# Large tiles at one SBUF offset, two places for queries, reordered first tiles, W_q's low parts on another engine, and the last residuals in the tokens' ring

## The chip, the cores and the metric

One core of one Trainium2 chip runs the kernel. The metric is the device time of one execution in microseconds (us). Engines are named as the profile names them: PE (TensorE matmuls), PEld (its weight loads), DVE (VectorE), ACT (ScalarE), POOL (GpSimd), SP (the queue that issues most DMAs).

## The reference

A conditioned linear attention over x of shape (2, 2048, 512), with 8 heads of 64 channels, all in float32:

```
xn = ln(x, ln_w, ln_b)
q = xn @ Wq + bq
k = xn @ Wk + bk + (1.0 - src_mask) * -1000000.0
q = softmax(q.reshape(b, t, h, dh), axis=-1)
k = softmax(k.reshape(b, t, h, dh), axis=1)
v = ((xn @ Wv + bv) * src_mask).reshape(b, t, h, dh)
att = einsum('bnhd,bnhl->bhdl', k, v)
y = einsum('bnhd,bhdl->bnhl', q, att).reshape(b, t, d)
scale, shift = split(silu(emb) @ W_emb + b_emb, 2)
hh = ln(y, ln2_w, ln2_b) * (1.0 + scale) + shift
out = x + silu(hh) @ W_out + b_out
```

## The kernel before

Tokens are worked in tiles of 128, 16 tiles for each of the two batch elements (b is 0 or 1, a tile of both together is m = 16 b + n). Four products take most of PE's time: K (`product_k`, normalised tokens by W_k), Q (`product_q`, by W_q), G (`product_g`, exponentials of the keys by masked tokens, summed over all tiles of a batch element) and O (`product_out`, the output). Each operand of them is split in a high and a low part of type float32r, and each product is three matmuls of 512 columns (high by high, high by low, low by high; L1154 to L1156), four times for a tile: 12 matmuls for each tile and product, 32 x 12 x 4 = 1,536 in all. A matmul has a stationary 128x128 block, loaded first, and a moving operand of 512 columns. In the profile's rows "ps<-wk_hi,zT_hi", the first name is what moves and the second what is stationary.

- K and Q: stationary `zT` (the turned tokens), moving `wk` or `wq`. 768 matmuls.
- G: stationary `zm` (masked tokens), moving `ek` (exponentials). 384 matmuls.
- O: moving `wo`; stationary `h`, which has no tiles of its own: below m = `HT` = 12 it stands in `zm` or `ek` (144 matmuls), from 12 on in `zT` when m % 4 is 0 or 1 (120) and in the tiles of `wk`, free by then, when m % 4 is 2 or 3 (120).

Besides, PE turns tiles (four 128x128 transposes of L1159 each), multiplies queries with the state (L1330) and sums exponentials (L1255).

The other engines: ACT makes normalised tokens, exponentials and high parts (`zT_high`, `ek_high`, `zm_high`, `h_high`, all by L306) and `scale_shift` (four pieces of L407 and a tanh, L412). DVE makes sums with biases, maxima, statistics and low parts (`q_add` L762, `q_top` L767, `k_less_max` L798, `masked_z` L779, `zm_low` L793, `ek_low` L803, `silu` L916, `out_tile` L922). POOL subtracts the maximum from queries (`q_shift` L577), makes `h_low` (L586) and adds b_out to the residual (`add_bias` L590).

Nothing schedules this at run time: every engine has its own list of instructions, in the order in which its code is written, and waits on semaphores. So an instruction that waits holds up all that stand behind it on its engine. The stages in order are: start (weights split while the first tokens come), K and Q of batch element 0, G of 0, a stage with K and Q of 1 beside the outputs 0 to 10, the turn to G of 1 (`k_less_max`, the last query tile, output 11), G of 1, and the outputs 12 to 31.

Details that the change touches:

- `qs`, the query tile between DVE, POOL and ACT, has one place: `q_add` waits for the exponential of the tile before (`dve.wait_ge(s["q_exp"], m)`).
- `product_g(b, 0)` writes four banks in the order 0, 2, 1, 3. Bank 1 waits for `q_sum` of the last query tile (the bank was that tile's), and for b = 1 bank 3 waits for `o_ok` of output 11 (`pe.wait_ge(s["o_ok"], HT)`), which is DVE's `out_tile(HT - 1)`, which needs POOL's `add_bias(HT - 1)`.
- Residuals stand in `res`, three places in turn: load, `add_bias`, `out_tile` adds the product in place, store, and only then the load of the tile three later (`refill`).
- Tiles of SBUF are given addresses in the order in which they are declared, each from a multiple of 32 bytes. In the program before, the weights (`wk_hi` to `wo_lo`) start 128 bytes past a multiple of 2,048 in each partition, `x_in`, `zT`, `kf` and `eq` 1,952 past one, `zm`, `ek`, `y`, `eqT`, `u`, `th`, `res` and `att` 2,016 past one.

Of the kernel before, what the change touches and what calls it, by code (L numbers as in the profile page):

```python
# [19 lines left out]
def cond_linear_attention(nc, x, cond, mask, ln_w, ln_b, wq, bq, wk, bk, wv, bv, w_emb, b_emb,  # L20
# [44 lines left out]
    with ExitStack() as ctx:  # L65
# [22 lines left out]
        part = sb("part", [P, P])  # L88
        ones = sb("ones", [P, 32])
# [7 lines left out]

        x_in = sb("x_in", [P, XR, D])  # L100
        zT_hi, zT_lo = sb("zT_hi", [P, 2, NB, P], F32R), sb("zT_lo", [P, 2, NB, P], F32R)

        kf = sb("kf", [P, T, D])
        eq = sb("eq", [P, T, D])
        qs = sb("qs", [P, D])
        qmax = sb("qmax", [P, H])
        km = sb("km", [P, D])
        kcol = sb("kcol", [P, NB])

        zm_hi, zm_lo = sb("zm_hi", [P, HI, D], F32R), sb("zm_lo", [P, LO, D], F32R)  # L110
        ek_hi, ek_lo = sb("ek_hi", [P, HI, D], F32R), sb("ek_lo", [P, LO, D], F32R)
        y = sb("y", [P, YR, D])
# [20 lines left out]
        yst_ps = [in_psum(yst[k], 64 * k) for k in range(2)]  # L133
        x_r, x_shift = sb("x_r", [P, T]), sb("x_shift", [P, T])
# [47 lines left out]
        def flat(t):  # L182
# [3 lines left out]
        wk_raw, wq_raw, wo_raw = y[:, 0:4], kf[:, 4:8], eq[:, 6:10]  # L186
        bias_part, bv_all = kf[:, 15, :], kf[:, 14, :]
# [9 lines left out]
            wk_hi_ok wk_lo_ok wq_hi_ok wq_lo_ok wv_ok wo_hi_ok wo_lo_ok  # L197
# [9 lines left out]
        res_in = [sem(f"res_in{t}") for t in range(RR)]  # L207
        stored = [sem(f"stored{t}") for t in range(RR)]
# [18 lines left out]
        def _(sp):  # L227
# [7 lines left out]

            def store(m):
                sp.wait_ge(s["o_ok"], m + 1)
                sp.dma_start(out_tok[:, m, :], res[:, m % RR, :]).then_inc(stored[m % RR], 16)

            def refill(m):  # L240

                if m >= 0 and m + RR < B * T:
                    sp.wait_ge(stored[m % RR], 16 * (m // RR + 1))
                    load_res(m + RR)
# [59 lines left out]
        def _(act):  # L304
# [26 lines left out]
            def exp_q(b, n):  # L331
# [4 lines left out]
                act.activation(eq[:, n, :], qs[:], ACT.Exp).then_inc(s["q_exp"], 1)  # L336
# [189 lines left out]
            scale_shift(HT)  # L526
            zm_high(1, 1)
            exp_k(1, 1)
            ek_high(1, 1)
            exp_q(1, T - 1)  # L530
            h_high(HT)
            scale_shift(HT + 1)

            def last_outputs(n):
                if n == 2:
# [32 lines left out]
        def _(pool):  # L568
# [19 lines left out]
            def add_bias(m):  # L588
                pool.wait_ge(res_in[m % RR], 16 * (m // RR + 1))
                pool.tensor_tensor(res[:, m % RR, :], res[:, m % RR, :], bo_all[:], ALU.add).then_inc(s["res_b"], 1)  # L590
# [61 lines left out]
        def _(dve):  # L652
# [850 lines left out]
```

## Time and profile before

| | |
|---|---|
| median of 3 runs | 483.63 us (482.94 to 485.74) |
| the profiled execution's own time | 484.99 us |
| its span, first to last instruction | 483.2 us |
| PE busy | 464.2 us (96%) |
| DVE busy | 363.3 us (75%) |
| ACT busy | 263.1 us (54%) |
| POOL busy | 132.8 us (27%) |
| mean granted clock of TensorE | 0.996 |

Busy time of PE counts each matmul to its modelled end, and consecutive ones overlap; so how fast PE runs is read from the starts of consecutive rows, not from the busy share.

### The profile page before, as it was taken

How to read it: one execution, taken by the hardware profiler on the slowest of the kernel's cores; microseconds unless marked ns; L12 is line 12 of the kernel's file. 1: busy time of each engine (PE TensorE's matmuls, PEld its weight loads, DVE VectorE, ACT ScalarE, POOL GpSimd, SP SyncE). 2: the span in 40 equal slices, each digit the busy share in tenths (PEclk: the TensorE clock that was granted, in tenths of full speed). 3: DMA queues.
4: the chain of work that ended last, by engine and by line, in shares of the span. 5: the costliest groups of instructions: out<-in, count | busy, mean ns of one | idle time of the engine just before them, and what ended most of it. 6: DMA issues, size and time to landing. Idle time of an engine off the chain costs nothing.

```text
span 483.2 us, 7324 instructions
## 1 busy us (share of the span) xinstructions
PE 464.2 (96%) x2478; PEld 371.8 (77%) x2478; DVE 363.3 (75%) x879; ACT 263.1 (54%) x485; POOL 132.8 (27%) x148
## 2 busy tenths in 40 slices
PE   4999999998899999999999999999899999989997
PEld 2677876885688878888888888888588868878875
DVE  6979976775878956979678658675988628888963
ACT  5333332321788523347555655655988814777882
POOL 0013311120200000104223233332410133676675
PEclk9999999999999999999999999999999999999999
DMA  8945310112133200110213212121322000233354
GB/s 284 356 168 207 121 43 7 46 46 102 43 121 98 88 26 19 45 43 1 82 28 132 84 49 87 45 87 45 131 85 69 0 1 23 89 131 124 123 172 149
DMA packets 23093, 43.50 MB, mean 90 GB/s; under 512 B 1992, under 2 KB 2064, under 8 KB 23056
## 3 DMA queue, kind: packets, MB, share of 16 engines
q1 hardware_dynamic: 21968, 40.93, 24.7%
q10 hardware_dynamic: 1088, 2.10, 1.2%
q8 instruction: 20, 0.33, 0.3%
q14 instruction: 17, 0.14, 0.1%
HBM read 34.64 MB, written 8.39 MB: 89 GB/s over the span
## 4 chain that ended last, share of the span: by engine, by line
PE 83%; DVE 8%; ACT 3%; issue 3%; POOL 1%; DMA 1%; POOLq 0%; DVEq 0%; ACTq 0%
PE ps L1154 21%; PE ps L1156 21%; PE ps L1155 21%; PE ps L1159 8%; PE ps L1330 5%; ACT ps L407 2%; PE ps L1255 1%; PE ps L1308 1%; DVE th L916 1%; PE ps L1227 1%; PE ps L1208 1%; DMA x_in<-in_x_dram 1%; DVE yst_raw L661 1%; DVE kf L798 1%; DVE qs L762 1%
## 5 line engine op out<-in xcount | busy, mean ns | idle before, releaser
L577 POOL TENSOR_TENSOR qs<-qs,qmax 128x512 f32<-128x512 f32 x32 | 35.9, 1122 | 192.8 <-DVE qmax L767 192.8
L1154 PE MATMUL ps<-ek_hi,zm_hi 128*128 128x512 f32 x128 | 51.5, 402 | 3.7 <-DVE ek_lo L803 2.1
L1154 PE MATMUL ps<-wk_hi,zT_hi 128*128 128x512 f32 x124 | 51.5, 415 | 1.7 <-DVE kf L748 1.7
L1154 PE MATMUL ps<-wq_hi,zT_hi 128*128 128x512 f32 x128 | 52.3, 409 | 0.3 <-DVE qs L762 0.3
L1156 PE MATMUL ps<-wq_hi,zT_lo 128*128 128x512 f32 x128 | 50.6, 395 | 0.0
L1155 PE MATMUL ps<-wq_lo,zT_hi 128*128 128x512 f32 x128 | 50.5, 395 | 0.0
L306 ACT ACTIVATE zT_hi<-ps 128x512 fp32r<-128x512 f32 x32 | 19.1, 596 | 57.6 <-PE ps L1159 57.6
L1156 PE MATMUL ps<-ek_hi,zm_lo 128*128 128x512 f32 x128 | 50.4, 394 | 0.0
L1155 PE MATMUL ps<-ek_lo,zm_hi 128*128 128x512 f32 x128 | 50.3, 393 | 0.0
L1156 PE MATMUL ps<-wk_hi,zT_lo 128*128 128x512 f32 x124 | 49.0, 395 | 0.0
L1155 PE MATMUL ps<-wk_lo,zT_hi 128*128 128x512 f32 x124 | 49.0, 395 | 0.0
L762 DVE TENSOR_TENSOR qs<-ps,bq_all 128x512 f32<-128x512 f32 x32 | 22.0, 689 | 32.9 <-PE ps L1156 30.5
L590 POOL TENSOR_TENSOR res<-res,bo_all 128x512 f32<-128x512 f32 x32 | 42.4, 1327 | 14.9 <-PE ps L1156 8.8
L306 ACT ACTIVATE eqT<-ps 128x512 f32<-128x512 f32 x17 | 10.2, 600 | 42.2 <-PE ps L1159 42.2
L1154 PEld LDWEIGHTS ps<-ek_hi,zm_hi 128*128 128x128 f32 x128 | 24.4, 191 | 11.0 <-DVE ek_lo L803 3.3
L748 DVE SCALAR_TENSOR_TENSOR kf<-ps,pen,bk_all 128x512 f32<-128x512 f32 x32 | 23.8, 746 | 11.6 <-PE ps L1156 11.5
L793 DVE TENSOR_TENSOR zm_lo<-x_in,zm_hi 128x512 fp32r<-128x512 f32 x32 | 22.6, 706 | 11.8 <-PE ps L1156 10.9
L922 DVE TENSOR_TENSOR res<-ps,res 128x512 f32<-128x512 f32 x32 | 21.9, 685 | 11.0 <-PE ps L1156 6.3
L336 ACT ACTIVATE eq<-qs 128x512 f32<-128x512 f32 x32 | 20.0, 625 | 17.3 <-POOL qs L577 17.3
L1154 PEld LDWEIGHTS ps<-wq_hi,zT_hi 128*128 128x128 f32 x128 | 24.1, 188 | 6.3 <-issue 0.8
L1156 PEld LDWEIGHTS ps<-wq_hi,zT_lo 128*128 128x128 f32 x128 | 24.0, 188 | 5.8
L1154 PEld LDWEIGHTS ps<-wk_hi,zT_hi 128*128 128x128 f32 x124 | 23.3, 188 | 6.6 <-issue 2.3
(230 smaller groups left out, 1163.2 us busy)
## 6 DMA issues: line engine op xcount, KB each, us to landing
x_in<-in_x_dram SPq DMA_DIRECT2D x32, 512.0 KB, 3.5
res<-in_x_dram SPq DMA_DIRECT2D x32, 256.0 KB, 2.8
out_dram<-res SPq DMA_DIRECT2D x32, 256.0 KB, 2.0
y<-in_L_cond_Wk_dram ACTq DMA_DIRECT2D x2, 512.0 KB, 5.3
kf<-in_L_cond_Wq_dram ACTq DMA_DIRECT2D x1, 1024.0 KB, 8.1
eq<-in_L_cond_W_out_dram SPq DMA_DIRECT2D x1, 1024.0 KB, 8.5
wv_mod<-in_L_cond_Wv_dram SPq DMA_DIRECT2D x1, 1024.0 KB, 10.7
eq<-in_L_cond_W_emb_dram SPq DMA_DIRECT2D x4, 256.0 KB, 4.4
```

Of the source, the lines that this page charges most:

```text
L306: act.activation(o, i, ACT.Copy, scale=scale).then_inc(s[done], 1)
L577: pool.tensor_tensor(q_heads, q_heads, qmax[:].unsqueeze(2).broadcast_to([P, H, DH]), ALU.subtract).then_inc(s["q_shift"], 1)
L590: pool.tensor_tensor(res[:, m % RR, :], res[:, m % RR, :], bo_all[:], ALU.add).then_inc(s["res_b"], 1)
L748: dve.scalar_tensor_tensor(out=kf[:, n, :], in0=ps[:, OB if m == 1 else KB, :], scalar=pen[:, m:m + 1], in1=bk_all[:], op0=ALU.add, op1=AL ...
L762: dve.tensor_tensor(qs[:], ps[:, TB if m == 1 else QB, :], bq_all[:], ALU.add).then_inc(s["q_sum"], 1)
L793: dve.tensor_tensor(zm_lo[:, n % LO, :], x_in[:, at, :], zm_hi[:, n % HI, :].bitcast(F32), ALU.subtract).then_inc(s["zm_lo_ok"], 1)
L922: dve.tensor_tensor(res[:, m % RR, :], o_bank(m), res[:, m % RR, :], ALU.add).then_inc(s["o_ok"], 1)
L1154: pe.matmul(o, a[0], bb[0], start=start, stop=False)
L1155: pe.matmul(o, a[0], bb[1], start=False, stop=False)
L1156: return pe.matmul(o, a[1], bb[0], start=False, stop=stop)
L1159: return pe.transpose(o, i, ident[0:i.shape[0], 0:i.shape[0]])
L1330: last = pe.matmul(ps[:, bank, at:at + YW], eqT[:, m % 2, q, :] if m < T else blk(eq[:, m - T, :], q), att[:, q, :], start=True, stop=True)
```

## The change

Six edits stand in the diff. The large tiles are declared ahead of the small ones, and `qs` grows by a tile, so that every large tile from `x_in` to `att` starts 1,152 bytes past a multiple of 2,048, and the weights stay at 128: all of them are 128 past a multiple of 1,024. `qs` and `qmax` have two places. The low parts of W_q are POOL's, which takes the scaled weight from ACT (`wq_scaled`, a second copy) and subtracts the high part; the statistics of tokens 2 to 5 stand in PSUM, in the bank of the queries, so the first query product waits for them. At the turn to G of batch element 1 and in the last outputs several steps stand in another order. In the start, `key_bias(1)` stands ahead of the first transposes. The residuals of outputs 24 to 31 are loaded in pairs into `x_in`, all at once when G is done, and stored from there.

```diff
+        x_in = sb("x_in", [P, XR, D])
+        zT_hi, zT_lo = sb("zT_hi", [P, 2, NB, P], F32R), sb("zT_lo", [P, 2, NB, P], F32R)
+        kf = sb("kf", [P, T, D])
+        eq = sb("eq", [P, T, D])
+        qs = sb("qs", [P, 2, D])
...
         ones = sb("ones", [P, 32])
...
-        qs = sb("qs", [P, D])
-        qmax = sb("qmax", [P, H])
+        qmax = sb("qmax", [P, 2, H])
...
+        xst_ps = in_psum(xst, 128)
...
+        def res_of(m):
+            return res[:, m % RR, :] if m < 2 * T - XR else x_in[:, m - 2 * T + XR, :]
...
+        wq_scaled = eq[:, 0:4]
...
+            sp.wait_ge(s["g_ps"], 2 * T)
+            for m in range(2 * T - XR, 2 * T, 2):
+                load_late(m)
             for m in range(HT, 2 * T):
                 store(m)
...
+            zT_high(0, 0)
             act.wait_ge(s["wk_in1"], 16)
             wk_high(2)
-            zT_high(0, 0)
             wk_high(3)
...
                 wq_high(f)
+                copy(wq_scaled[:, f, :], wq_raw[:, f, :], "wq_scaled", ln_weight(f))
...
+            for f in range(NB):
+                pool.wait_ge(s["wq_scaled"], f + 1)
+                pool.tensor_tensor(wq_lo[:, f, :], wq_scaled[:, f, :], wq_hi[:, f, :].bitcast(F32),
+                                   ALU.subtract).then_inc(s["wq_lo_ok"], 1)
...
-                if m:
-                    dve.wait_ge(s["q_exp"], m)
+                if m > 1:
+                    dve.wait_ge(s["q_exp"], m - 1)
...
             masked_z(1, 0)
             k_less_max(1, 0)
+            masked_z(1, 1)
+            k_less_max(1, 1)
             out_tile(HT - 2)
-            k_less_max(1, 1)
             zm_low(1, 0)
             q_add(1, T - 1)
             ek_low(1, 0)
             q_top(1, T - 1)
-            masked_z(1, 1)
+            out_tile(HT - 1)
+            zm_low(1, 1)
+            ek_low(1, 1)
             k_less_max(1, 2)
             masked_z(1, 2)
             silu(HT)
-            out_tile(HT - 1)
-            zm_low(1, 1)
-            ek_low(1, 1)
...
+            silu(T + 2)
             out_tile(HT + 3)
...
+                if m == 0:
+                    pe.wait_ge(s["x_norm"], 2)
...
             key_bias(0)
+            key_bias(1)
             turn_z(0, 0)
             turn_z(0, 1)
-            key_bias(1)
```

On ACT the same turn has `scale_shift(HT)` behind `ek_high(1, 1)` in place of ahead of `zm_high(1, 1)`, and `h_high(HT)`, `scale_shift(HT + 1)` and `h_high(HT + 1)` move from the turn into steps 1, 3 and 5 of G.

**First place, the turn to G of batch element 1, on DVE.** The list starts at the maximum of the keys (`kcol`). `x_in<-x_in` is `masked_z`, `kf<-kf,ps` is `k_less_max`, `res<-ps,res` is `out_tile`, `th<-th,u` is `silu`. Before:

```order
L779 TENSOR_SCALAR x_in<-x_in,xm_r,xm_shift 128x512
L798 TENSOR_TENSOR kf<-kf,ps 128x512
L779 TENSOR_SCALAR x_in<-x_in,xm_r,xm_shift 128x512
L916 SCALAR_TENSOR_TENSOR th<-th,u 128x512
L922 TENSOR_TENSOR res<-ps,res 128x512
L793 TENSOR_TENSOR zm_lo<-x_in,zm_hi 128x512
L803 TENSOR_TENSOR ek_lo<-kf,ek_hi 128x512
```

In the changed program, from `q_top` of the last query tile on:

```order
L801 TENSOR_REDUCE qmax<-qs 128x8
L956 TENSOR_TENSOR res<-ps,res 128x512
L827 TENSOR_TENSOR zm_lo<-x_in,zm_hi 128x512
L837 TENSOR_TENSOR ek_lo<-kf,ek_hi 128x512
L832 TENSOR_TENSOR kf<-kf,ps 128x512
L813 TENSOR_SCALAR x_in<-x_in,xm_r,xm_shift 128x512
L950 SCALAR_TENSOR_TENSOR th<-th,u 128x512
```

`out_tile(11)` and the low parts of state tile 1 moved ahead of `k_less_max` and `masked_z` of tile 2 and of `silu(12)`.

**Second place, the last outputs, on DVE**, around output 15 (`res<-ps,res`) and output 18's `silu` (`th<-th,ps`). Before:

```order
L862 TENSOR_TENSOR kf<-ps,rec 128x512
L922 TENSOR_TENSOR res<-ps,res 128x512
L661 BN_STATS yst_raw<-kf 128x6 x2
L916 SCALAR_TENSOR_TENSOR th<-th,ps 128x512
L858 RECIPROCAL rec<-ps 128x8
```

and in the changed program:

```order
L896 TENSOR_TENSOR kf<-ps,rec 128x512
L950 SCALAR_TENSOR_TENSOR th<-th,ps 128x512
L956 TENSOR_TENSOR res<-ps,res 128x512
L693 BN_STATS yst_raw<-kf 128x6 x2
L892 RECIPROCAL rec<-ps 128x8
```

`silu(18)` moved ahead of `out_tile(15)` and of two statistics.

## Rows read from the trace of the kernel before

**Rows 1.** The page, part 1: busy time, share of the span, instructions.
```profile
PE 464.2 (96%) x2478; PEld 371.8 (77%) x2478; DVE 363.3 (75%) x879; ACT 263.1 (54%) x485; POOL 132.8 (27%) x148
```

**Rows 2.** The page, part 4: the chain that ended last, by engine.
```profile
PE 83%; DVE 8%; ACT 3%; issue 3%; POOL 1%; DMA 1%; POOLq 0%; DVEq 0%; ACTq 0%
```

**Rows 3.** Timeline of PE: start, duration (us); a K product, then G.
```profile
55.02 0.39 PE L1155 MATMUL ps<-wk_lo,zT_hi 128*128 128x512 f32 x1
...
57.34 0.40 PE L1156 MATMUL ps<-wk_hi,zT_lo 128*128 128x512 f32 x1
...
139.76 0.39 PE L1155 MATMUL ps<-ek_lo,zm_hi 128*128 128x512 f32 x1
...
144.97 0.39 PE L1154 MATMUL ps<-ek_hi,zm_hi 128*128 128x512 f32 x1
```

**Rows 4.** Timeline of PE: matmuls 2 and 12 of three O products.
```profile
434.10 0.40 PE L1155 MATMUL ps<-wo_lo,wk_hi 128*128 128x512 f32 x1
...
436.41 0.40 PE L1156 MATMUL ps<-wo_hi,wk_lo 128*128 128x512 f32 x1
...
438.21 0.39 PE L1155 MATMUL ps<-wo_lo,zT_hi 128*128 128x512 f32 x1
...
440.54 0.40 PE L1156 MATMUL ps<-wo_hi,zT_lo 128*128 128x512 f32 x1
...
477.20 0.40 PE L1155 MATMUL ps<-wo_lo,wk_hi 128*128 128x512 f32 x1
...
479.47 0.39 PE L1156 MATMUL ps<-wo_hi,wk_lo 128*128 128x512 f32 x1
```

**Rows 5.** Timeline, start of G of batch element 0; in brackets idle before.
```profile
124.68 0.69 DVE L762 TENSOR_TENSOR qs<-ps,bq_all 128x512 f32<-128x512 f32 x1 [1.67 <-ACT eq L336]
...
125.43 0.50 PE L1154 MATMUL ps<-ek_hi,zm_hi 128*128 128x512 f32 x1 [0.69 <-DVE qs L762]
...
129.82 0.68 DVE L803 TENSOR_TENSOR ek_lo<-kf,ek_hi 128x512 fp32r<-128x512 f32 x1
...
130.55 0.50 PE L1154 MATMUL ps<-ek_hi,zm_hi 128*128 128x512 f32 x1 [0.73 <-DVE ek_lo L803]
```

**Rows 6.** Timeline, turn to G of batch element 1.
```profile
343.52 1.49 POOL L590 TENSOR_TENSOR res<-res,bo_all 128x512 f32<-128x512 f32 x1
...
346.21 0.50 PE L1154 MATMUL ps<-ek_hi,zm_hi 128*128 128x512 f32 x1 [0.96 <-DVE res L922]
...
346.68 1.77 DVE L803 TENSOR_TENSOR ek_lo<-kf,ek_hi 128x512 fp32r<-128x512 f32 x1
...
348.50 0.79 PE L1154 MATMUL ps<-ek_hi,zm_hi 128*128 128x512 f32 x1 [1.33 <-DVE ek_lo L803]
...
352.10 0.40 PE L1154 MATMUL ps<-ek_hi,zm_hi 128*128 128x512 f32 x1
```

**Rows 7.** Windows 349:350: busy PE, PEld, DVE, ACT, POOL; granted clock; DMA.
```profile
349.00:350.00 1.00, 1.00 (x4) 0.71 (x4) 0.70 (x3) 1.00 (x3) 0.00 (x0) 0.50 1.05 408
```

**Rows 8.** Timeline, the last outputs, around output 18's `silu`.
```profile
421.15 0.60 ACT L412 ACTIVATE th<-ps 128x512 f32<-128x512 f32 x1
...
424.31 0.67 DVE L916 SCALAR_TENSOR_TENSOR th<-th,ps 128x512 f32<-128x512 f32 x1
...
428.39 0.66 PE L1159 MATMUL ps<-ident,kf 128*128 128x128 f32 x4 [1.55 <-ACT kf L395]
```

**Rows 9.** Timeline, the start of the kernel.
```profile
9.21 1.97 PE L1159 MATMUL ps<-ident,x_in 128*128 128x128 f32 x8 [0.66 <-ACT x_in L321]
...
21.94 0.50 PE L1154 MATMUL ps<-wq_hi,zT_hi 128*128 128x512 f32 x1
```

**Rows 10.** Groups by line, POOL: busy us, mean ns.
```profile
L623 POOL TENSOR_TENSOR wo_lo<-eq,wo_hi 128x512 fp32r<-128x512 f32 x4 | 5.2, 1298 | 0.0
```

**Rows 11.** Timeline, the stall in the fifth token tile.
```profile
42.65 0.48 PE L1154 MATMUL ps<-wk_hi,zT_hi 128*128 128x512 f32 x1 [0.70 <-DVE kf L748]
```

**Rows 12.** Timeline, the end.
```profile
480.00 0.69 DVE L922 TENSOR_TENSOR res<-ps,res 128x512 f32<-128x512 f32 x1 [1.15 <-POOL res L590]
```

More of the change, by code:

```diff
@@ L88, in cond_linear_attention @@
         part = sb("part", [P, P])
+        x_in = sb("x_in", [P, XR, D])
[3 more added lines that the diff above has]
+        qs = sb("qs", [P, 2, D])
+        km = sb("km", [P, D])
+        zm_hi, zm_lo = sb("zm_hi", [P, HI, D], F32R), sb("zm_lo", [P, LO, D], F32R)
+        ek_hi, ek_lo = sb("ek_hi", [P, HI, D], F32R), sb("ek_lo", [P, LO, D], F32R)
+        y = sb("y", [P, YR, D])
+        eqT = sb("eqT", [P, 2, NB, P])
+        u, th = sb("u", [P, D]), sb("th", [P, D])
+        res = sb("res", [P, RR, D])
+        att = sb("att", [P, NB, YW])
         ones = sb("ones", [P, 32])
@@ L207, in cond_linear_attention @@
         res_in = [sem(f"res_in{t}") for t in range(RR)]
+        res_late = [sem(f"res_late{t}") for t in range(XR // 2)]
         stored = [sem(f"stored{t}") for t in range(RR)]
@@ L234, in load_res, with load_late @@
                 sp.dma_start(res[:, m % RR, :], x_tok[:, m, :]).then_inc(res_in[m % RR], 16)
+            def load_late(m):
+                at = m - 2 * T + XR
+                sp.dma_start(x_in[:, at:at + 2, :], x_tok[:, m:m + 2, :]).then_inc(res_late[at // 2], 16)
             def store(m):
                 sp.wait_ge(s["o_ok"], m + 1)
[L238 removed]
+                sp.dma_start(out_tok[:, m, :], res_of(m)).then_inc(stored[m % RR], 16)
             def refill(m):
[L242 removed]
+                if m >= 0 and m + RR < B * T - XR:
                     sp.wait_ge(stored[m % RR], 16 * (m // RR + 1))
@@ L335, in exp_q @@
                     act.wait_ge(s["eqT_ps"], n + 1)
-                act.activation(eq[:, n, :], qs[:], ACT.Exp).then_inc(s["q_exp"], 1)
+                elif n < NB:
+                    act.wait_ge(s["wq_lo_ok"], n + 1)
+                act.activation(eq[:, n, :], qs[:, n % 2, :], ACT.Exp).then_inc(s["q_exp"], 1)
             def exp_k(b, n):
@@ L529, in _ @@
             ek_high(1, 1)
+            scale_shift(HT)
             exp_q(1, T - 1)
-            h_high(HT)
-            scale_shift(HT + 1)
             def last_outputs(n):
-                if n == 2:
+                if n == 1:
+                    h_high(HT)
+                if n == 3:
+                    scale_shift(HT + 1)
+                if n == 5:
                     h_high(HT + 1)
@@ L588, in add_bias @@
             def add_bias(m):
-                pool.wait_ge(res_in[m % RR], 16 * (m // RR + 1))
-                pool.tensor_tensor(res[:, m % RR, :], res[:, m % RR, :], bo_all[:], ALU.add).then_inc(s["res_b"], 1)
+                if m < 2 * T - XR:
+                    pool.wait_ge(res_in[m % RR], 16 * (m // RR + 1))
+                else:
+                    pool.wait_ge(res_late[(m - 2 * T + XR) // 2], 16)
+                pool.tensor_tensor(res_of(m), res_of(m), bo_all[:], ALU.add).then_inc(s["res_b"], 1)
             steps_done = [0]
@@ L696, in xst_of @@
             def xst_of(b, c):
+                if b == 0 and c == 1:
+                    return xst_ps
                 return yst[0] if b and c == 0 else xst
```

36 lines of the change are left out of this document (11 added, 25 removed).

## Prediction

> **What bounds the kernel now.** I read the busy times first: PE is busy for 96% of the span, DVE for 75% [rows 1]. Then the chain that ended last: 83% of it lies on PE and 8% on DVE [rows 2]. So two things can shorten the kernel: a smaller distance between PE's matmuls, and the removal of places where PE stands still. For the first I read the timeline of PE, from start to start inside a product, since busy time overlaps. For the second I went through the timeline for rows of PE that carry an idle time.
>
> **The distance between matmuls.** In a K product ten steps take 57.34 - 55.02 = 2.32 us, 0.232 each; in G 23 steps take 144.97 - 139.76 = 5.21 us, 0.2265 each [rows 3]. Both are 128x128 by 512 columns of the same type. In the outputs the same code runs with the stationary operand in two places: out of `zT` ten steps take 2.33 us (0.233), out of `wk` 2.31 (0.231) in a slow product and 2.27 (0.227) in a fast one [rows 4]. What differs is where the tiles stand. `wk` and `wo` start at the same byte modulo 2,048, and so do `zm` and `ek`, the pair of G; `zT` and the weights do not. So rows of one kernel, one of them with nothing else changed, say that a pair at the same offset is faster by 2 to 6 ns. The change gives every pair the same offset modulo 1,024. Blocks inside a tile lie 512 bytes apart, so `wk` by `wo` products already contain distances of 512, 1,024 and 1,536 bytes; a distance of 1,024 is nothing new.
>
> Of the 1,536 matmuls 384 (G) and 120 (O out of `wk`) have equal offsets already. 1,032 are left; I leave out 24 of the fifth token tile, where PE waits for DVE [rows 11], and 24 of outputs 28 and 29, which are paced by ACT and DVE. I take the middle of the fast and the slow product, 0.229, against 0.233: 984 x 0.004 = **3.9 us**. The ends are 984 x 0.002 = 2.0 and 984 x 0.006 = 5.9.
>
> The Trainium skill speaks against this term. "TensorE: Matmul & The Clock Gate", section "Step-by-step: what each phase is for", says that PE reads the moving operand and the weights through two independent ports, so that loading weights takes no read bandwidth from a running matmul; by that rule where the tiles stand changes nothing and the term would be 0. The rows show a difference by place, so I give that rule a rival and not the forecast.
>
> **Two places for queries.** At the start of G of batch element 0, `q_add` of the last query tile waited 1.67 us for the exponential of the tile before, and PE's bank 1 waited 0.69 us for it [rows 5]. With two places it waits for the exponential two tiles back, long done, so it goes as soon as its product is there, which PE finishes before it begins G, six matmuls ahead of bank 1. So PE's wait of 0.69 goes, 0.8 with the restart, and its start moves from 125.43 to about 124.6. Behind it on DVE everything comes some 1.5 us sooner, `ek_low` of tile 2 too, which PE awaited for 0.73 us [rows 5]. With PE 0.8 sooner as well, `ek_low`'s end of 130.5 has to come to 128.8; its chain (`k_less_max` on DVE, exponential and two high parts on ACT) comes 1.3 to 1.6 sooner. I take 1.5 of the 1.7 us: **1.5 us**. The ends are 0.8 (the second stall stays) and 1.7.
>
> **The turn to G of 1.** Before, PE waited 0.96 us for `out_tile(11)`, ran three matmuls and waited 1.33 us for `ek_low(1)`, which took 1.77 us where other rows of its kind take 0.68 [rows 5, 6]. Then PE's granted clock was 0.50 [rows 7], its lower level of 1.2 GHz, after 0.96 + 1.33 us of idleness: from 348.50 to 352.10 there are nine matmuls, 3.60 us in place of 9 x 0.227 = 2.04, a loss of 1.56. In the new order `out_tile(11)` stands right behind `q_top`, but it also needs POOL's `add_bias(11)`, which ended at 343.52 + 1.49 = 345.01 [rows 6] and stands behind `q_shift` of the last query tile, hence behind `q_top`, which is now half a microsecond later for the `masked_z(1)` ahead of it. DVE is then idle, so POOL's two instructions should run at their undisturbed lengths and give most of that back. So `out_tile` starts at 345.1 to 345.4, PE goes on at about 345.9 (0.3 sooner), `zm_low(1)` and `ek_low(1)` follow at 0.6 to 0.7 each and end at 347.1, and `product_g(1, 1)` starts at 347.15 in place of 348.50: 1.35. The clock should hold, since the idle stretches shrink to 0.75 and 0.5 us: 1.56 more. What is late next is tile 2: its `k_less_max`, `masked_z`, `silu(12)` and `k_less_max(3)` now stand behind, then ACT's chain; I find `ek_low(2)` ending at 350.5, when PE wants it at 349.8, and a rest of 0.35 at tile 3, where the statistics' steps moved to steps 1 to 4. So 1.35 + 1.56 - 1.05 = **1.9 us**. The ends are 0 (the wait on POOL grows and the clock falls again) and 3.8, when no new wait comes.
>
> The Trainium skill, "SBUF — State Buffer", section "Who interferes with whom", says that a VectorE instruction with two SBUF inputs and a GpSimd instruction that reads SBUF exclude each other. The 1.77 us row agrees: POOL's `h_low(12)` ran beside it. By that rule `ek_low(1)` is free of it in the new order, since `silu(12)` comes later; a `silu` that is held up costs PE nothing there.
>
> **The last outputs.** Tanh of output 18 ended at 421.75, its `silu` ran at 424.31, and the chain from there through ACT (high part, `scale_shift`, `normalise_y`) let PE wait 1.55 us at 428.39 [rows 8]. `silu` moves ahead of three instructions, 1.8 us sooner, and PE finds its transpose ready. But the next `silu` then stands behind `out_tile(16)`, which waits for PE, and ACT is 0.9 us late for the transpose after it. I take **1.0 us**; the ends are 0.6 and 1.7.
>
> **The start.** `key_bias(1)` fills PE's idle 0.66 us [rows 9], and product K of tile 0 starts some 0.8 sooner; its third and fourth blocks wait for weights that ACT now makes later. I take **0.5 us**, ends 0 and 0.8. W_q's low parts cost nothing: ACT adds four copies of some 0.64 us between those of `wq_high`, which I let begin at 13.7, so the last is ready by 18.8; POOL subtracts four times at 1.3 [rows 10], over by 20.3, and PE's first query product came at 21.94 [rows 9]. The cover is 1 us; if it is gone, each late microsecond is one of PE's. The same holds for the new wait on the statistics, which I put at 20.4, since DVE is rid of four instructions. The DVE stall of 0.70 in the fifth tile stays [rows 11]: DVE is released by PE ahead of it, so its lead is lost.
>
> **The late residuals** are worth 0. Loads that waited for stores delayed `add_bias`, but at the end DVE's last sum began at 480.00 [rows 12] while PE's last matmul had started at 479.47 [rows 4] and lasted 0.39. Four more issues on SP before output 12's store lie in the sum of exponentials.
>
> **Sum.** 3.9 + 1.5 + 1.9 + 1.0 + 0.5 = 8.8 us. The profiled execution took 484.99 us (span 483.2), and would take 476.2. It lies 1.36 above the median of the runs, so for the median I predict 483.63 - 8.8 = **474.8 us**.
>
> **The rivals.**
> - The offset does nothing (the port rule above): gain 4.9, 478.7 us. For it: G stands in another stage, and a product's distance differs by 4 ns among products of the same pair. Against it: outputs out of `zT` and `wk` alternate in one stage. Chance 0.15.
> - The turn to G of 1 gains nothing, as DVE's list now stands still behind POOL: gain 6.9, 476.7 us. Chance 0.14. Both together and a late W_q leave less than 2.4: chance 0.05.
> - Everything at the fast end, with all pairs at 0.227: 5.9 + 1.7 + 3.8 + 1.7 + 0.8 = 13.9, 469.7 us. Chance 0.05.
> - Slower: the wait on POOL at the turn leaves PE's clock at 0.50 for much of G. At that level a matmul takes 0.427 in place of 0.227, so 47% of the time is lost. To end 2.4 us above before it has to eat 6.9 + 2.4 = 9.3 us, that is 20 us at half clock, against 3.3 before. Nothing in the rows shows such a stretch; PE works without a gap from the third tile on. Chance 0.03.
>
> The forecast itself has 0.58.
>
> **The numbers.** The range goes from 471.0 (most of the fast case left out) to 478.8, which takes in the first two rivals. A measurement here tells about 0.5% (2.4 us) from no change: faster by more than that 0.92, within it 0.05, slower 0.03.
>
> **What would show it.** K, Q and `zT` outputs at 0.227 to 0.231 from start to start; no idle PE row at bank 1 of `product_g(0, 0)`; no stretch at clock 0.50 in G of 1, but one wait of 0.7 us or so for `out_tile(11)` and one for `ek_low(2)`; the 1.55 us row gone and one of 0.9 in its place one output later. Distances of 0.233 in K and Q would make the largest term wrong, and a first query product later than 21.4 the one on W_q.

## Result and the profile after

The kernel before took 483.52 us in the median of 4 runs (482.94 to 485.74), the changed one 479.27 us (4 runs, 478.93 to 480.19). The ratio is 0.991, with a 95% interval of 0.9884 to 0.9937. So the change gained 4.3 us (0.6 to 1.2% by the interval) where I had forecast 8.8: the direction was right, the size was not, and the time lies outside my range (471.0 to 478.8). A second measurement of the same kernel beside others (e13 below) gave 479.32.

First the page after, parts 1 and 4, which answer to [rows 1, 2].

```profile
PE 459.6 (96%) x2478; PEld 369.9 (77%) x2478; DVE 359.7 (75%) x875; ACT 264.8 (55%) x489; POOL 137.4 (29%) x152
...
PE 80%; DVE 11%; issue 4%; ACT 2%; DMA 1%; POOL 0%; ACTq 0%; DVEq 0%
```

PE lost 4.6 us of busy time with the same number of matmuls. Some 1.6 of it is the stretch at half clock [rows 7], which is not there after the change; the rest says that a matmul got cheaper. But DVE's part of the chain rose from 8% to 11%, so PE waits for DVE in a new place. The timeline of PE in the changed kernel (start, duration, in brackets the idle time ahead and who ended it) shows where:

```profile
8.37 3.75 PE L1245 MATMUL ps<-y,cols 128*128 128x512 f32 x4 [3.89 <-DMA y<-in_L_cond_Wk_dram]
...
23.14 0.50 PE L1188 MATMUL ps<-wq_hi,zT_hi 128*128 128x512 f32 x1
...
118.92 0.60 PE L1193 MATMUL ps<-ident,kcol 128*128 128x128 f32 x4
...
128.83 0.50 PE L1188 MATMUL ps<-ek_hi,zm_hi 128*128 128x512 f32 x1 [0.21 <-DVE ek_lo L837]
...
333.00 0.65 PE L1193 MATMUL ps<-ident,kcol 128*128 128x128 f32 x4 [0.35 <-DVE kcol L806]
...
337.80 0.47 PE L1188 MATMUL ps<-wo_hi,ek_hi 128*128 128x512 f32 x1 [1.40 <-DVE res L956]
...
344.47 0.50 PE L1188 MATMUL ps<-ek_hi,zm_hi 128*128 128x512 f32 x1 [0.23 <-DVE ek_lo L837]
...
347.93 0.50 PE L1188 MATMUL ps<-ek_hi,zm_hi 128*128 128x512 f32 x1 [0.45 <-DVE ek_lo L837]
...
352.07 0.50 PE L1188 MATMUL ps<-ek_hi,zm_hi 128*128 128x512 f32 x1 [1.08 <-DVE ek_lo L837]
...
396.49 2.03 PE L1367 MATMUL ps<-att,eq 128*128 128x130 f32 x16 [0.30 <-ACT eq L324]
...
423.35 0.60 PE L1193 MATMUL ps<-ident,kf 128*128 128x128 f32 x4
...
474.80 0.39 PE L1190 MATMUL ps<-wo_hi,wk_lo 128*128 128x512 f32 x1
```

The reader is to see three things. At the start of G of batch element 0 the row at bank 1 [rows 5] is gone and the second stall shrank from 0.73 to 0.21. The wait of 1.55 us in the last outputs [rows 8] is gone. And at the turn to G of 1 the two waits of [rows 6] gave way to four: 1.40, 0.23, 0.45 and 1.08. The first of them is new, and DVE and POOL of the same kernel show what it is made of:

```profile
334.88 1.29 POOL L615 TENSOR_TENSOR ek_lo<-th,ek_hi 128x512 fp32r<-128x512 f32 x1 [5.76 <-ACT ek_hi L324]
...
335.10 1.35 DVE L813 TENSOR_SCALAR x_in<-x_in,xm_r,xm_shift 128x512 f32<-128x512 f32 x1
...
336.98 0.68 DVE L956 TENSOR_TENSOR res<-ps,res 128x512 f32<-128x512 f32 x1
...
340.12 1.05 POOL L606 TENSOR_TENSOR qs<-qs,qmax 128x512 f32<-128x512 f32 x1 [3.96 <-DVE qmax L801]
...
341.13 1.29 POOL L622 TENSOR_TENSOR res<-res,bo_all 128x512 f32<-128x512 f32 x1
...
342.52 0.69 DVE L956 TENSOR_TENSOR res<-ps,res 128x512 f32<-128x512 f32 x1 [2.48 <-POOL res L622]
...
344.93 0.55 DVE L813 TENSOR_SCALAR x_in<-x_in,xm_r,xm_shift 128x512 f32<-128x512 f32 x1
...
349.83 1.64 POOL L615 TENSOR_TENSOR zT_lo<-th,zT_hi 128x512 fp32r<-128x512 f32 x1 [7.40 <-ACT zT_hi L324]
...
350.24 1.78 DVE L837 TENSOR_TENSOR ek_lo<-kf,ek_hi 128x512 fp32r<-128x512 f32 x1
```

`out_tile(10)` (336.98) now stands behind `masked_z(1, 1)` (335.10) and a `k_less_max`, and PE's `product_out(11)` writes the bank that `out_tile(10)` has to read first. More than half of the wait of 1.40 comes from the length of `masked_z(1, 1)`: it took 1.35 us beside POOL's `h_low(11)` (334.88), where the next one (344.93), with nothing on POOL, took 0.55. The clock did hold, as I had said; the window that answers to [rows 7]:

```profile
349.00:350.00 1.00, 1.00 (x6) 0.82 (x5) 0.90 (x6) 1.00 (x3) 0.17 (x1) 1.00 0.00 0
```

To add the gains up I cut PE's timeline at five rows that every kernel has: its first bias product (6.51 us before), the turn of `kcol` of batch element 0 (119.13 before), the first product out of `att` (184.86), the turn of `kcol` of 1 (336.42), the first product out of `att` behind it (399.82), and the end of the last matmul.

| stretch of PE, us | before | after | difference |
|---|---|---|---|
| up to the first bias product | 6.51 | 8.37 | +1.86 |
| to `kcol` of 0 (start, K, Q) | 112.62 | 110.55 | -2.07 |
| to `att` of 0 (G of 0) | 65.73 | 64.12 | -1.61 |
| to `kcol` of 1 | 151.56 | 149.96 | -1.60 |
| to `att` of 1 (the turn, G of 1) | 63.40 | 63.49 | +0.09 |
| to the end (outputs) | 80.04 | 78.70 | -1.34 |
| end of the last matmul | 479.86 | 475.19 | -4.67 |

The first line is the landing of W_k's first half, 1.9 us later in this execution than in the one before; whether that is chance is taken up below.

### The profile page after: what moved, and what is told of

Read it like the earlier page. It is cut to its first block, busy times and chain, and to the rows that moved or that the text cites. A ratio compares the mean times of both kernels' runs of the same rounds, so it can differ in the third digit from the quotient of the medians.

```text
span 478.4 us, 7328 instructions
## 1 busy us (share of the span) xinstructions
PE 459.6 (96%) x2478; PEld 369.9 (77%) x2478; DVE 359.7 (75%) x875; ACT 264.8 (55%) x489; POOL 137.4 (29%) x152
## 4 chain that ended last, share of the span: by engine, by line
PE 80%; DVE 11%; issue 4%; ACT 2%; DMA 1%; POOL 0%; ACTq 0%; DVEq 0%
PE ps L1188 21%; PE ps L1190 21%; PE ps L1189 20%; PE ps L1193 8%; PE ps L1367 4%; PE ps L1292 1%; DMA y<-in_L_cond_Wk_dram 1%; PE ps L1245 1%; DVE kf L896 1%; DVE res L956 1%; DVE ek_lo L837 1%; ACT ps L428 1%; PE ps L1345 1%; PE ps L1264 1%; DVE th L950 1%
## 5 line engine op out<-in xcount | busy, mean ns | idle before, releaser
L622 POOL TENSOR_TENSOR res<-res,bo_all 128x512 f32<-128x512 f32 x24 | 31.6, 1319 | 11.8 <-PE ps L1190 8.8
L775 DVE TENSOR_TENSOR zT_lo<-ps,zT_hi 128x512 fp32r<-128x512 f32 x32 | 21.9, 686 | 8.5 <-ACT zT_hi L324 8.5
```

Source lines behind the costliest of these rows:

```text
L622: pool.tensor_tensor(res_of(m), res_of(m), bo_all[:], ALU.add).then_inc(s["res_b"], 1)
L775: dve.tensor_tensor(flat(zT_lo[:, n % 2]), z_bank(T * b + n), flat(zT_hi[:, n % 2]).bitcast(F32), ALU.subtract).then_inc(s["zT_lo_ok"], 1)
```

## The experiments

Times are medians of 4 to 12 runs, but e5, e6, e12, e15 and e16 ran once each. Every kernel was run beside the kernel before on the same chip, whose median was 483.6 to 484.6 us; the changed kernel itself was not run beside the others except in e13. So where two medians of different experiments lie within 1.5 us, I go by the stretches of PE's timeline. They repeat within 0.2 us from kernel to kernel wherever neither the code, the offsets nor the clock differ, except the first, which holds the start.

**e1: the order of declarations alone.** The kernel before with the new order of `sb(...)` lines and nothing else.

```diff
+        x_in = sb("x_in", [P, XR, D])
+        zT_hi, zT_lo = sb("zT_hi", ...), sb("zT_lo", ...)
...
         ones = sb("ones", [P, 32])
...
-        x_in = sb("x_in", [P, XR, D])
```

> The kernel before with only the declaration order of the tiles changed, so that all large tiles stand 128 bytes past a multiple of 1,024. If the offset is worth what the starts of matmuls in the changed kernel say (3.5 to 5 ns on about 1,000 matmuls), 479.6 us, and K, Q and zT outputs at 0.229 from start to start. If the pitch fell for another reason, 483.5 us and 0.233. For the start: if the new places make W_k's load slower, its first half lands at about 8.3 us; if that was chance of one run, at about 6.4.

Measured: 480.01 us, ratio 0.9924 (0.9896 to 0.9952), a gain of 3.9 us (2.3 to 5.0 by the interval). The offsets alone are worth most of the measured gain. In PE's timeline, from the first Q product on and without the stretch that holds the turn, they are worth 1.41 + 0.07 + 1.44 + 0.04 = 3.0 us against before. The stretch to `att` of 1 took 62.39 us here, with the old lists at the turn; that is 1.0 shorter than before and after.

**e2: everything but the order of declarations.** A filler of 32 bytes behind `qs` restores the old offsets although `qs` has grown.

```diff
-        x_in = sb("x_in", [P, XR, D])
+        ones = sb("ones", [P, 32])
```

> The changed kernel with the tiles at their old offsets. Offset theory: all other edits together are worth about 0.4 to 1 us, so 482.5 to 483 us, pitch 0.233 in K and Q. Rival, that the offset gives nothing: 479.3 us. W_k lands at about 6.4 us if the layout made it late in the changed kernel, at either time if it is chance.

Measured: 481.98 us, ratio 0.9955 (0.9938 to 0.9971), 1.9 us below before. Together with e1's 3.9 that would be 5.8, more than the whole change gained; with the 3.0 of the timeline it is 4.9. Its stretches were 111.70, 64.19, 151.57, 63.52 and 78.84: G of 0 and the outputs as after, the others longer by 1.15 and 1.61.

**e3: the sum of output 10 first again.** The changed kernel with one instruction of DVE moved.

```diff
+            out_tile(HT - 2)
             masked_z(1, 1)
             k_less_max(1, 1)
-            out_tile(HT - 2)
```

> The changed kernel with out_tile(10) again ahead of masked_z(1, 1) and k_less_max(1, 1). PE's wait of 1.40 us ahead of output 11's product should go. Theory that the turn hangs on POOL's add_bias(11) behind q_shift behind q_top: the time stays within 0.4 us of the changed kernel (479.3), since PE then waits for bank 3 some 1.4 us longer. Rival, that out_tile(10) alone cost the turn: 477.9 us.

Measured: 477.78 us, ratio 0.9868 (0.9842 to 0.9895). That is 1.5 us below the changed kernel and near the rival's 477.9, and my expectation that the time would come back at POOL was wrong. But the timeline does not bear the rival out in full, since the greater part of the 1.40 came back at ACT:

```profile
330.75 0.65 PE L1193 MATMUL ps<-ident,kcol 128*128 128x128 f32 x4 [0.35 <-DVE kcol L806]
...
338.22 0.63 PE L1193 MATMUL ps<-ident,y 128*128 128x128 f32 x4 [1.24 <-ACT u L428]
...
345.08 0.50 PE L1188 MATMUL ps<-ek_hi,zm_hi 128*128 128x512 f32 x1 [0.40 <-DVE ek_lo L837]
...
349.21 0.50 PE L1188 MATMUL ps<-ek_hi,zm_hi 128*128 128x512 f32 x1 [1.10 <-DVE ek_lo L837]
```

The wait of 1.40 at `product_out(11)` is gone and another of 1.24 stands behind that product: `turn_y(13)` wants the scratch `u`, and ACT's `scale_shift(12)` was moved behind three instructions of tile 1 by the change. In the changed kernel it was hidden under the wait of 1.40. The stretch to `att` of 1 shortened by only 0.6 (to 62.88). The other 0.9 is not in the turn; the first bias product came at 5.96 here against 8.37, so it may be the landing of the weights. That isn't shown.

**e4: POOL's bias ahead of its query shift.** e3, and:

```diff
                 if t == T - 1:
                     h_low(HT - 1)
+                    add_bias(HT - 1)
                 q_shift(1, t)
-            add_bias(HT - 1)
```

> As the kernel with out_tile(10) first, and POOL's add_bias(11) ahead of q_shift of the last query tile. Theory of the POOL chain: out_tile(11) follows its product, PE has no wait at bank 3, product_g(1, 1) starts 2 us sooner, and the POOL subtract that slowed ek_low(3) lies elsewhere: 476.3 to 477.3 us. Rival, that DVE's own list bounds the turn: 478.5 to 479.3 us.

Measured: 476.50 us, ratio 0.9844 (0.9814 to 0.9873). The time is as expected, and the stretch to `att` of 1 fell by 1.55 to 61.33. One part of the expectation failed: `ek_low(3)` still took 1.78 us beside POOL's `h_low(12)`.

**e7: ACT's `scale_shift(12)` ahead of tile 1 again.** e4, and:

```diff
+            scale_shift(HT)
             zm_high(1, 1)
             exp_k(1, 1)
             ek_high(1, 1)
-            scale_shift(HT)
```

> The kernel of e4 with ACT's scale_shift of output 12 back ahead of masked z's high part of tile 1, so that it ends at some 337.2 and not 338.8. First theory: PE's wait of 1.19 us for u of output 12 goes, but DVE has no idle row from there to ek_low of tile 3, so PE only meets that wait (0.63) grown to 1.4 to 1.8; gain over e4 0 to 0.4 us, 476.1 to 476.5. Rival: the wait is simply removed and everything behind it comes 1.2 us sooner, 475.3.

Measured: 476.35 us, ratio 0.9849 (0.9828 to 0.9869), the stretch to `att` of 1 61.30 against 61.33. The wait for `u` is gone, and nearly all of it came back as `ek_low`'s:

```profile
21.32 0.50 PE L1188 MATMUL ps<-wq_hi,zT_hi 128*128 128x512 f32 x1 [0.62 <-DVE x_shift L725]
...
344.11 0.50 PE L1188 MATMUL ps<-ek_hi,zm_hi 128*128 128x512 f32 x1 [0.40 <-DVE ek_lo L837]
...
348.24 0.50 PE L1188 MATMUL ps<-ek_hi,zm_hi 128*128 128x512 f32 x1 [1.11 <-DVE ek_lo L837]
```

(The first row belongs to the start, and comes up below.) In e4 the row that answers to the second has no idle time and the one that answers to the third 0.63. So by then DVE sets the pace of the turn, as a window of e4 (busy PE, PEld, DVE, ACT, POOL, then the clock) says in one figure, 7.00 of 7.00 us:

```profile
338.00:345.00 7.00, 6.07 (x29) 5.14 (x30) 7.00 (x12) 5.67 (x12) 1.04 (x1) 1.00 0.44 151
```

**e8: work out of DVE's way.** e7, with the four parts of `y_finish` on DVE and the high parts and `scale_shift` on ACT some tiles later:

```diff
-                if 1 <= n < 5:
-                    y_finish(T - 1, (n - 1,))
+                if 3 <= n < 7:
+                    y_finish(T - 1, (n - 3,))
...
-                if n == 1:
+                if n == 3:
                     h_high(HT)
-                if n == 3:
+                if n == 4:
                     scale_shift(HT + 1)
-                if n == 5:
+                if n == 6:
                     h_high(HT + 1)
```

> The kernel of e7 with work moved out of DVE's way in the first tiles of G of 1: the four parts of y_finish at tiles 3 to 6 and the high part of output 12 at tile 3, so that POOL's low part runs beside a later ek_low. If DVE's list is what bounds these tiles, the wait at tile 3 shrinks to below 0.4 us and the time is 1.0 to 1.5 us below e4 (475.0 to 475.5); if the contention with POOL only moves to a later tile and PE then waits there, it is the same as e7.

Measured: 476.29 us, ratio 0.9849 (0.9826 to 0.9873). In the profile the wait of 1.11 is gone, `ek_low` of tile 3 (347.29) took 0.69 us, and the stretch to `att` of 1 is 60.84, 0.46 below e7:

```profile
343.56 0.50 PE L1188 MATMUL ps<-ek_hi,zm_hi 128*128 128x512 f32 x1 [0.42 <-DVE ek_lo L837]
```

The medians don't tell e8 from e7, so the gain that I expected of it (1.0 to 1.5) isn't there; the trace shows 0.5.

**e9: the old lists at the turn.** The changed kernel with DVE's and ACT's lists of before at the turn to G of 1, the rest as changed; the part on DVE:

```diff
-            masked_z(1, 1)
-            k_less_max(1, 1)
             out_tile(HT - 2)
+            k_less_max(1, 1)
...
-            out_tile(HT - 1)
-            zm_low(1, 1)
-            ek_low(1, 1)
+            masked_z(1, 1)
...
             silu(HT)
+            out_tile(HT - 1)
+            zm_low(1, 1)
+            ek_low(1, 1)
```

> The changed kernel with the lists of ACT and DVE at the turn to G of 1 as they were before; the rest of the change stays. My prediction gave the new lists 1.9 us, by which this takes 481.2. The theory after the profiles: from the turn's transpose of kcol to the exponentials' sums it took 63.4 us with the new lists (after and e2), 62.4 with the old ones where no stretch at clock 0.50 came (e1) and 63.4 where it came (before). So the new lists cost 1.1 us in an ordinary run, and this takes 478.2. Rival: the old lists profit from neither, 479.3 as after.

Measured: 478.29 us, ratio 0.9868 (0.9841 to 0.9895). That is 1.0 us below the changed kernel (479.3), where my prediction had the new lists gain 1.9. The interval overlaps that of e13 (0.9868 to 0.9918), so the time alone rules out the gain but does not fix the cost; the stretches, 63.49 with the new lists and 62.39 with the old ones in e1, put it at 1.1. The profiled execution had the two old waits and behind them the low clock:

```profile
340.40 0.50 PE L1186 MATMUL ps<-ek_hi,zm_hi 128*128 128x512 f32 x1 [1.00 <-DVE res L954]
...
342.68 0.79 PE L1186 MATMUL ps<-ek_hi,zm_hi 128*128 128x512 f32 x1 [1.32 <-DVE ek_lo L835]
```

```profile
344.00:345.00 1.00, 1.00 (x4) 0.72 (x4) 1.00 (x3) 1.00 (x3) 0.00 (x0) 0.50 0.43 166
```

and its stretch to `att` of 1 took 63.52. In e1, with the same lists, the window just behind the stall reads

```profile
344.00:345.00 1.00, 0.78 (x3) 0.67 (x4) 0.76 (x2) 1.00 (x4) 0.00 (x0) 1.00 1.01 391
```

and the stretch took 62.39, although PE had stood for as long:

```profile
341.94 0.50 PE L1152 MATMUL ps<-ek_hi,zm_hi 128*128 128x512 f32 x1 [1.02 <-DVE res L920]
...
344.22 0.50 PE L1152 MATMUL ps<-ek_hi,zm_hi 128*128 128x512 f32 x1 [1.30 <-DVE ek_lo L801]
```

The six runs of e9 say the same of one program: three had a mean clock of 0.996 (477.85 to 479.20 us) and three of 0.999 or 1.000 (477.50 to 478.92). So the same lists fall to 0.50 in some executions and not in others.

**e10: the start of before.** W_q's low parts by DVE in place of POOL, no copies on ACT, `key_bias(1)` behind the two turns, and `x_finish(0, 1)` in its old place.

```diff
-                copy(wq_scaled[:, f, :], wq_raw[:, f, :], "wq_scaled", ln_weight(f))
...
+                weight_low(wq_lo, wq_raw, wq_hi, "wq", f)
...
-                if m == 0:
-                    pe.wait_ge(s["x_norm"], 2)
...
-            key_bias(1)
             turn_z(0, 0)
             turn_z(0, 1)
+            key_bias(1)
```

> The changed kernel with the start as it was: W_q's low parts by DVE from the raw weights, ACT without its four copies, key_bias(1) behind the two turns, the old place of the second chunk's statistics. My prediction gave the start 0.5 us: 479.8. By the profiles from PE's first bias product to the turn of kcol 0 the start is worth 0.6 to 0.9 us: 479.9 to 480.2. Rival: PE then waits for the statistics (0.6 us in e7) or W_q's parts as long as it gained, 479.3.

Measured: 478.70 us, ratio 0.9881 (0.9853 to 0.991). Not slower than the changed kernel, so the forecast gain of 0.5 is not there.

**e11: `silu` of output 18 back.**

```diff
-            silu(T + 2)
             out_tile(HT + 3)
...
-                if T < m < 2 * T - 2:
+                if m + 2 < 2 * T:
                     silu(m + 2)
```

> The changed kernel with the silu of output 18 back behind the sum of output 15. My prediction gave that step 1.0 us (0.6 to 1.7); by the profile of after the stretch of the outputs became 1.3 us shorter, so the time is 480.6. Rival: the wait is given back at the next output anyway, 479.3.

Measured: 480.03 us, ratio 0.9907 (0.9879 to 0.9934), 0.7 us above the changed kernel on other chips, and 1.3 above e10 on the same one. The times don't fix the size. The old wait is back, and the stretch of the outputs is 79.90 against 78.70:

```profile
423.31 0.66 PE L1192 MATMUL ps<-ident,kf 128*128 128x128 f32 x4 [1.57 <-ACT kf L416]
```

**e13 and e14: the changed kernel again, and e8 with the start of before.** e13 has no edit, and e14 is e8 with the edit of e10.

> The changed kernel itself, beside the others on the same chip. If the late landing of the first half of W_k (PE's first bias product at 8.37 us) was that execution's alone, the profile starts at 6 to 7.5 us and the median is 478.8 to 479.0; if it belongs to the change, it starts after 8 again and the median is 479.3.

> The kernel of e8 with the start of before, as in e10. If the new start is worth the predicted 0.5 us, it takes 476.8; if it gains nothing, 476.3; if PE's new wait for the statistics makes it cost 0.5, 475.8.

Measured: e13 479.32 us, ratio 0.9893 (0.9868 to 0.9918); e14 476.81 us, ratio 0.9845 (0.9819 to 0.9871), where e8 had 0.9849. With the start of before the best kernel is as fast as with the new one. In e13 PE's first bias product again came late, and the median is the one that I had named for a late landing that belongs to the change:

```profile
8.06 3.75 PE L1245 MATMUL ps<-y,cols 128*128 128x512 f32 x4 [3.32 <-DMA y<-in_L_cond_Wk_dram]
```

**e5, e6, e12, e15, e16: how equal the offsets must be.** The changed kernel with 32, 64, 512, 128 and 256 bytes of padding, which move `zT`, `zm` and `ek` together against the weights:

```diff
         part = sb("part", [P, P])
+        gap = sb("gap", [P, 8])
```

> The changed kernel with 32 bytes of padding ahead of x_in, so that zT, zm and ek stand 32 bytes away from the weights modulo 64, as they did before, while everything else about the new layout stays. If the phase modulo 64 bytes between the stationary and the moving tile is what costs, the start-to-start distance in K, Q and outputs by zT, zm or ek returns to 0.233 us (0.2292 after the change) and G, whose two tiles move together, stays at 0.2275; the time is about 3.9 us longer than after the change, near 483. If only larger distances (512 bytes and up) matter, the distances stay at 0.229.

> The same with 64 bytes of padding. If the phase modulo 64 bytes is what costs, all distances stay at 0.229 and the time at about 479.3. If the tiles must agree modulo 512 or 1,024 bytes, as my prediction put it, they return to 0.233 in K, Q and the outputs, and the time is near 483.

> The changed kernel with 512 bytes of padding ahead of x_in, one block's distance inside a tile. Products of wk and wo contain distances of 512, 1,024 and 1,536 bytes between the two operands and run at 0.229. If equality modulo 512 bytes is enough, K, Q and the outputs stay at 0.229 and the time at 479.3. If it is modulo 1,024, they return to 0.233 and the time to about 482, as with 32 and 64 bytes.

> The changed kernel with 128 bytes of padding ahead of x_in. If equality modulo 128 bytes is enough, K, Q and the outputs stay at 0.229 from start to start; if it takes 256 or 512, they are at 0.233.

> The same with 256 bytes. With e15 it brackets the step: 0.229 here and 0.233 in e15 is 256 bytes, 0.233 in both is 512, 0.229 in both is 128.

One product's distance varies (0.226 to 0.233 after the change), so I read the stretch from the first matmul of tile 0's Q product to the turn of `kcol`, which holds the 360 matmuls of tiles 1 to 15 and some others. The two rows of each kernel, with 64 bytes (e6), 128 (e15), 256 (e16) and 512 (e12):

```profile
21.58 0.50 PE L1189 MATMUL ps<-wq_hi,zT_hi 128*128 128x512 f32 x1
...
118.84 0.60 PE L1194 MATMUL ps<-ident,kcol 128*128 128x128 f32 x4
```

```profile
21.33 0.51 PE L1189 MATMUL ps<-wq_hi,zT_hi 128*128 128x512 f32 x1
...
118.44 0.60 PE L1194 MATMUL ps<-ident,kcol 128*128 128x128 f32 x4
```

```profile
21.56 0.50 PE L1189 MATMUL ps<-wq_hi,zT_hi 128*128 128x512 f32 x1
...
117.36 0.60 PE L1194 MATMUL ps<-ident,kcol 128*128 128x128 f32 x4
```

```profile
22.45 0.50 PE L1189 MATMUL ps<-wq_hi,zT_hi 128*128 128x512 f32 x1
...
118.20 0.60 PE L1194 MATMUL ps<-ident,kcol 128*128 128x128 f32 x4
```

| kernel | distance modulo 256 bytes | stretch, us | K products, start to start | time, us |
|---|---|---|---|---|
| before | 32 | 97.19 | 0.2328 | 483.5 |
| e2 | 32 | 97.19 | 0.2330 | 481.98 |
| e5 | 32 | 97.17 | 0.2327 | 481.95 |
| e6 | 64 | 97.26 | 0.2334 | 482.09 |
| e15 | 128 | 97.11 | 0.2326 | 481.23 |
| e16 | 0 (256) | 95.80 | 0.2301 | 478.92 |
| e12 | 0 (512) | 95.75 | 0.2300 | 479.69 |
| after | 0 | 95.78 | 0.2293 | 479.3 |
| e1 | 0 | 95.78 | 0.2300 | 480.01 |

There is nothing between the two levels. Equality modulo 256 bytes is enough; an offset of half of that is as bad as one of 32. The three padded kernels with unequal offsets took 1.9 to 2.8 us more than the changed one, which fits a term of 3.0 better than one of 3.9.

Two rows of pairs that the padding moves together or not at all speak against other readings. G, whose two tiles move together, kept a median of 0.226 to 0.227 through all five paddings, so it is not where a tile stands by itself. And outputs out of `wk`, which alternate with those out of `zT` in one stage, kept 0.229 to 0.230 in e5, e6 and e15, while those out of `zT` went to 0.232 and 0.233.

## Why the prediction was wrong

**The offset (3.9 us): right in its cause, and a little large.** e1 gained 3.9 us, and the distances fell by 3.6 to 5.1 ns in Q and in the outputs out of `zm`, `ek` and `zT` (0.2330 to 0.2291, 0.2343 to 0.2292, 0.2335 to 0.2288, 0.2331 to 0.2295). G and the outputs out of `wk` did not move, as forecast. In PE's stretches the same term, after against e2, is 1.15 + 0.07 + 1.61 + 0.03 + 0.14 = 3.0 us, as between e1 and before. So that e1's median met the forecast to the tenth is partly luck: the product of matmuls and nanoseconds comes out whole only where PE sets the pace, and the outputs behind `att`, with 120 of the matmuls that I counted, gave only 0.14 of their 0.5. The rival of the two ports (0.15) is out. The Trainium skill says in "TensorE: Matmul & The Clock Gate", section "Step-by-step: what each phase is for", that the two operands have ports of their own. What I drew from it for the rival, that places then change nothing, e1, e6 and e16 do not bear out: 64 bytes of padding cost 1.5 us in 97. Where in the chip the two operands meet no run here shows. Of my description one piece was off: I spoke of equality modulo 1,024 bytes, and 256 are enough.

**Two places for queries (1.5 us): right.** G of 0 became 1.61 us shorter, and in e1, which has one place, it stayed at 65.66. The row at bank 1 went and the second stall shrank to 0.21, as written. No run has this edit alone; the size is read from the timeline.

**The turn to G of 1 (+1.9 us): this step failed.** The stretches show a cost of 1.1 in place of a gain of 1.9 (63.49 with the new lists, 62.39 with the old ones at full clock), and e9's time agrees with 1.0. Two errors are in it.

The first is of cause: the waits and the path were wrong. I followed `out_tile(11)` and never asked who waits for `out_tile(10)`, which the same edit put behind `masked_z(1, 1)` and `k_less_max(1, 1)`. PE's next product writes its bank, so PE stood for 1.40 us (e3 took that wait away), and behind it stood another of 1.24 for the scratch `u`, from ACT's list (e3, e7). Nor did POOL's undisturbed lengths give the time back. `q_top` came later by more than the half microsecond that I gave `masked_z(1, 1)`, since that one ran beside `h_low(11)` at 1.35 us; POOL's `add_bias(11)` ended 9.42 us behind the turn of `kcol` (341.13 + 1.29 - 333.00), against 8.59 before. With `add_bias(11)` ahead of `q_shift` the stretch lost 1.55 us at once (e4).

In the terms of my sum, all from the turn of `kcol` and with e1 for the old lists: `product_g(1, 1)` started 0.60 us sooner (11.47 against 12.07), where I had 1.35. The waits at tiles 2 and 3 were 0.45 and 1.08, where I had 0.7 and 0.35, and cost 1.70 with what hangs on them (52.02 us from there to `att` against 50.32), where I had 1.05. That is 0.60 - 1.70 = -1.1. The larger of the two waits is there since POOL's `h_low(12)`, moved with the rest, now ran beside `ek_low(3)` (1.78 us at 350.24). So the contention was moved, not removed. The trace still agrees with the rule that I named from the Trainium skill ("SBUF — State Buffer", section "Who interferes with whom"): it is again the DVE instruction with two SBUF inputs that took 1.78 in place of 0.68, and in e8 the one at 347.29, with no POOL instruction beside it, took 0.69. What I had not counted with is `masked_z`, which reads one tile of SBUF: it took 1.35 or 1.36 in place of 0.55 in every kernel with the changed order.

The second error is of accounting: 1.56 of the 1.9 us was the clock of 0.50 [rows 7], which is not in the median that I subtracted from. Of 46 runs of the kernel before in these experiments 17 had a mean clock of 0.996 or less and took 484.8 to 487.3 us (median 485.7); the other 29, at 0.999 or 1.000, took 482.7 to 484.6 (median 483.6). The profiled execution was of the first kind (0.996, 484.99 us). I had written that it lay 1.36 above the median and had not put the two together. Where the low clock comes, the stretch with the old lists is 63.40 (before) and 63.52 (e9) against 62.39 (e1), so it costs 1.0 to 1.1 us there and not 1.56; what else the 17 runs lost I did not follow. All 61 runs of kernels with the new lists, or with variants of them, had a mean clock of 0.999 or 1.000, which helps in a third of the executions of the kernel before and not in the median.

**The last outputs (1.0 us): right, and a little larger.** The stretch behind `att` fell by 1.34, of which e2 against after puts 0.14 to the offsets, and e11 gave 1.20 back in the stretch. The wait of 0.9 that I expected one output later did not come: behind that place PE's rows have idle times of 0.41 and 0.16.

**The start (0.5 us): this step failed too, by its size.** PE's way from the first bias product to the first Q product took 14.0, 13.9 and 14.4 us with the old start (e1, e10, e14; 15.4 in the profile of before) and 14.2 to 15.5 with the new one, 14.8 in most; by times e10, e14 and e8 put it at nothing. W_q's low parts did not hold PE up. My sign for that, a first query product later than 21.4, did come (23.14), but no idle time stands ahead of it and the first bias product was 1.9 late. The new wait on the statistics, which I had counted as covered, does stand in the way in three of the fourteen profiles with the new start: 0.62 us in e7 (the row at 21.32), 0.59 in e11 and 0.28 in e4. What eats the gain in the others is not known.

**Sum.** With what was measured, offset 3.0 to 3.9, queries 1.6, turn -1.1, outputs 1.2, start 0, the change is worth 4.7 to 5.6 us, against 4.3 and 4.65 timed. From the first Q product to the end of the last matmul PE took 457.92 us before and 452.05 after; without the 1.0 of the low clock that is 4.8 or 4.9, so the lower end of the sum is the one that the timeline bears out. Of the missing 4.5 us the turn is 3.0, the start 0.5, and the offset 0.9. My second rival, that the turn gains nothing (0.14), was nearer the truth than the forecast.

**What stays open.** Whether the landing of W_k's first half belongs to the change in part. PE's first bias product came at 8.37 and 8.06 in the two profiles of the changed kernel and at 5.86 to 7.83 in the sixteen of all others, twelve of which have the same start. They are the two latest of eighteen, and by e13's expectation that speaks for the change; that no edit of the start separates them speaks for chance. Neither is shown. Both executions were also the slowest of their sets (480.19 of 4 runs, 480.12 of 6), so the medians need not hold all of it. It could be what the sum is over the time.

## What to carry to other kernels

When an edit puts an instruction behind others, list every engine that waits for it, and for all the ones it was moved behind and past, not only for the one that the edit is about: here `out_tile(10)` made PE wait for 1.40 us, which was in nobody's sum. Before a term of the profiled execution is subtracted from a median, look whether the median's runs contain it; the mean granted clock of each run tells. And a wait that goes is worth what the next one leaves: the 1.24 us for `u` were seen only when the 1.40 were gone (e3), and when the wait for `u` went too, those for `ek_low` grew from 0.63 to 0.40 + 1.11 (e7). The best kernels of the study, e4, e7 and e8, are 7.3 us below before (ratios 0.9844 to 0.9849), and two moved instructions (e4) make 2.8 us of it by the medians, 2.2 in the stretch of the turn.

## What the runs showed of the hardware

- The start-to-start distance of 128x128 by 512-column fp32r matmuls depends on where the two operands stand: 0.227 to 0.231 us when their byte offsets in SBUF are equal modulo 256 (after, e1, e12, e16), 0.232 to 0.234 when they differ by 32, 64 or 128 (before, e2, e5, e6, e15), or by 96 (outputs out of `zm` and `ek` before). It is a step, not a slope.
- G has a median of 0.226 to 0.227 in every kernel and the other pairs with equal offsets means of 0.228 to 0.231. What makes the rest of that difference is not known from these runs.
- Behind idle stretches of 1.00 and 1.32 us PE's clock fell to 1.2 GHz (0.50) for about 3 us in the profile of e9, behind 0.96 and 1.33 in that of before, and not at all behind 1.02 and 1.30 in that of e1. In e9 three of six runs, and in before 17 of 46, had the lower mean clock.
- DVE's `masked_z` (TENSOR_SCALAR, 128x512) took 1.35 us beside POOL's `h_low(11)` and 0.55 without; `ek_low` (TENSOR_TENSOR, two SBUF inputs) 1.78 beside `h_low(12)` and 0.68 without.
- PE's first product out of a loaded weight starts between 5.9 and 8.4 us after the span's start in programs with the same start; the 2.5 us between them are 0.5% of this kernel.
